# Eight-layer kernel on one core: three stretches reordered (start of the first layer, second expert layer with the attention behind it, last layer)

## The chip, the core and the metric

The kernel runs on one core of one Trainium2 chip, as one launch. Times are device microseconds of that core. The hardware profiler gives the busy time of each engine: TensorE (PE; PEld is its weight load), VectorE (DVE), ScalarE (ACT), GpSimd (POOL) and the queue that issues the transfers (SP).

## The reference

The input is 8 sequences of 256 tokens by 128 channels, float32. Eight layers are applied, each as `x = x + layernorm(f(layernorm(x)))`, with another f each time:

```python
f0: attention with a decaying prefix sum over cos/sin features (first layer, L0 attn)
f1: 8 experts, top 2, silu-gated                                (L0 ffn)
f2: 16-head softmax attention, with biases                      (L1 attn)
f3: (gelu(x @ W1[7] + b1[7]) @ W2[7] + b2[7]) * softmax(x @ Wr.T)[:, 7]      (L1 ffn)
f4: 16-head causal attention, polynomial in place of softmax    (L2 attn)
f5: a short attention over the sequences, then 8 experts, top 2, with a capacity (L2 ffn)
f6: causal softmax attention with one shared key head           (L3 attn)
f7: 16 experts in 4 groups: sigmoid scores; the 2 best groups by the sum of their 2 best
    scores; the 4 best experts in them, shares divided by their sum; silu(x@w1)*(x@w3)
    times the share, @ w2; plus a shared expert of width 128     (L3 ffn)
```

The three changed stretches are the start of f0, all of f3 with the start of f4, and all of f7. Everything is computed in float32, apart from the attention scores, whose operands are split into bf16 parts.

## The kernel before, in words

**Data.** `X` holds all tokens in SBUF, as 16 tiles of 128 tokens; a unit is one sequence, two tiles (T = 2), and there are NB = 8 units. All weights are loaded once at the start by SP, one pack per layer (`w_const`, `w_l0a`, `w_l0f`, ...; line 377), in this order: the first 4 tiles of X, const, l0a, the other 12 tiles of X, the bf16 constants in float32 (`cbf`, into PT), then the other packs.

**A unit of a layer.** The head: VectorE takes statistics of X (lines 1601 and 1604, semaphore hd_stat), GpSimd makes the inverse deviation (lines 395 and 397, hd_rstd), VectorE writes the normed state h (line 1611, hd_h), TensorE transposes it (line 896, hd_tr), ScalarE copies it out of PSUM (hd_hT). The layer's own work ends in an unnormed result. The tail: statistics (1617, 1620), GpSimd's inverse deviation again, the norm (1626) and the add to X (1629, semaphore x_done). Heads run one unit ahead.

**Order.** There is no scheduler: each engine has its own program, written out by hand, and runs it in order; semaphores, counted from the start, tie them together. A layer begins on TensorE once the last add of the layer before it is done (`pe.wait_ge(x_done, 1 + tail0[l])`). On VectorE every result that the next instruction reads needs an explicit `drain()` between.

**Start of the first layer.** GpSimd sets constants and clears the buffers of all the attentions (lines 405 to 420) and then raises `consts`, for which VectorE waits before its first statistics. VectorE norms unit 0, waits for the rest of X and for cbf, casts cbf (1702), then prepares the convolution weights `wcv` (1707 and 1712), the query weights `wab` (1709 to 1720), theta (1722) and the slopes, with one semaphore a_w for both weights. TensorE then runs the convolution (934) and the queries (943). VectorE computes exponents (1734, 1736) and angles (1742 to 1747), ScalarE copies the query factors (607), exponentiates (613) and takes sine and cosine (598 to 601), GpSimd multiplies them by the weights (551), TensorE makes running sums (957).

**Second expert layer (L1 ffn).** A hardware loop over the units on each engine. Only expert 7 is computed: hidden width 512 as two chunks of two 128-wide blocks. Per unit TensorE runs up(0), up(1) (line 1531, 256 columns each), then the transposes of the next unit's h, then down(0) and down(1) (line 1570) into one PSUM bank, and the next unit's router (1508). ScalarE does gelu (862), two copies of the next state (876, 879) and the exp of the router (845). VectorE begins with the next unit's h (1611), waits for down, adds the bias (2487), multiplies by the share (2491), takes the tail statistics, the head statistics of the unit behind, the router's maximum (1641, 1643), adds to X, and normalises the shares.

**Start of the third attention (L2 attn).** Behind the last add: projection of unit 0 (1241), loads from PSUM (1931 to 1933), and the splits of keys and queries into bf16 parts on VectorE (316 to 322, 332 to 338), their transposes (1248), copies, and the first scores (1266, 1255). In the loop of this attention GpSimd makes the splits.

**Last layer (L3 ffn).** A hardware loop again; five chunks per unit: chunk 0 the shared expert (width 128), chunks 1 to 4 four routed experts each. Per chunk TensorE runs up (1531), ScalarE silu (856), VectorE the product `y` (2437), TensorE the transposes of the spread shares `cwx` in PT (1542, function share), VectorE the product with the shares (2442), TensorE down (1570). The slots y, sg and the PSUM banks are doubled. The routing of the next unit stands between them on VectorE: sigmoid (2359, 2361), group scores (2364 to 2373), choice of groups (1668 to 1679, 2380 to 2388), comparison of 16 by 16 (1668 to 1674, 512 columns each), rank and shares (1679, 1682, 2394 to 2400, `cwn`). ScalarE spreads cwn over 64 columns each (871).

## Time and profile before

| | us |
|---|---|
| median of 3 runs | 1575.2 (1574.66 to 1577.04) |
| profiled execution, its own time | 1575.53 |
| its span | 1573.7 |
| TensorE busy in the span | 1217.3 |
| VectorE busy in the span | 1083.6 |
| ScalarE busy in the span | 737.8 |
| GpSimd busy in the span | 403.1 |

### The profile page before, as it was taken

Reading aid. Unit: us, or ns where it says so; the run is one execution under the profiler, and the core shown is the slowest. Engines: PE = TensorE matmul, PEld = TensorE weight load, DVE = VectorE, ACT = ScalarE, POOL = GpSimd, SP = SyncE. Lnnn points to the kernel's source line nnn. Section 1 sums busy time; section 2 is a strip of 40 time slices with the busy share of each in tenths; the row PEclk is TensorE's granted clock in tenths of the full one; section 3 lists DMA queues with packets and bytes.
Section 4 is the critical chain, followed back from the end, with each engine's and each line's share of the span. In section 5 each row is a group of like instructions: output and inputs, shape, how many; then the busy total and the mean of one; then the engine's idle time right before and its main releaser. Section 6 shows DMA issues by size and latency. Waiting matters only on the chain.

```text
span 1573.7 us, 27547 instructions
## 1 busy us (share of the span) xinstructions
PE 1217.3 (77%) x9120; PEld 853.1 (54%) x9120; DVE 1083.6 (69%) x3043; ACT 737.8 (47%) x1200; POOL 403.1 (26%) x622
## 2 busy tenths in 40 slices
PE   3989889999868777665678774877778999867876
PEld 2666658888733333454344442766663444456765
DVE  4788766666666777345788985788745666467777
ACT  3544523332326677553677772434233666524332
POOL 3545431000023332111545422222102223000000
PEclk8999989999958999777888995899886999969888
DMA  7000000000000000000000000000000000000000
GB/s 310 1 1 1 1 1 1 0 0 0 0 1 2 1 0 2 1 0 0 1 2 0 2 1 0 1 1 1 1 1 0 2 1 1 1 1 0 0 0 27
DMA packets 5688, 14.39 MB, mean 9 GB/s; under 512 B 224, under 2 KB 4448, under 8 KB 5088
## 3 DMA queue, kind: packets, MB, share of 16 engines
q1 hardware_dynamic: 5600, 13.26, 2.2%
q8 instruction: 49, 0.80, 0.2%
q14 instruction: 39, 0.32, 0.1%
HBM read 12.21 MB, written 1.05 MB: 8 GB/s over the span
## 4 chain that ended last, share of the span: by engine, by line
issue 51%; PE 20%; DVE 14%; POOL 5%; DVEq 4%; ACT 4%; POOLq 2%; DMA 1%; SPq 0%; ACTq 0%
PE PS L1116 3%; PE PS L1064 2%; PE PS L1058 2%; PE PS L1041 2%; POOL trs L397 2%; PE PS L1286 2%; PE PS L934 1%; DVE mx L1840 1%; POOLq L396 1%; DVE w_l0f L1950 1%; DVE sbuf L1747 1%; PE PS L957 1%; DVE h L1611 1%; PE PS L1022 1%; DVEq L1744 1%
## 5 line engine op out<-in xcount | busy, mean ns | idle before, releaser
L1840 DVE TENSOR_REDUCE mx<-PS 128x2 f32<-128x512 f32 (+1 forms) x256 | 155.0, 620 | 80.7 <-PE PS L1064 72.0
L672 ACT ACTIVATE w_l0f<-PS 128x512 f32<-128x512 f32 (+1 forms) x256 | 137.3, 543 | 100.4 <-PE PS L1071 97.7
L395 POOL TENSOR_TENSOR tve<-tmv,eps 128x2 f32<-128x2 f32 x64 | 12.6, 196 | 660.1 <-DVE tmv L1620 556.6
L856 ACT ACTIVATE sg<-PS 128x512 f32<-128x512 f32 (+1 forms) x104 | 60.4, 580 | 205.1 <-PE PS L1531 204.9
L1531 PE MATMUL PS<-hT_padded,w_l0f 128*128 128x256 f32 x512 | 121.7, 384 | 0.0
L896 PE MATMUL PS<-w_const,h 128*128 128x128 f32 x128 | 30.8, 328 | 104.5 <-DVE h L1611 95.0
L2437 DVE TENSOR_TENSOR y<-sg,PS 128x512 f32<-128x512 f32 (+1 forms) x104 | 69.3, 666 | 59.2 <-ACT sg L856 47.1
L1531 PEld LDWEIGHTS PS<-hT_padded,w_l0f 128*128 128x128 f32 x512 | 94.3, 193 | 10.8
L896 PEld LDWEIGHTS PS<-w_const,h 128*128 128x128 f32 x128 | 15.2, 154 | 126.7 <-DVE h L1611 86.0
L1531 PE MATMUL PS<-hT_padded,w_l3f 128*128 128x256 f32 x288 | 80.2, 432 | 0.0
L1444 PEld LDWEIGHTS PS<-w_l2f,y 128*128 128x128 f32 x512 | 72.0, 206 | 13.6 <-ACT y L789 8.8
L1444 PE MATMUL PS<-w_l2f,y 128*128 128x128 f32 x512 | 74.2, 292 | 6.5 <-ACT y L789 6.0
L1950 DVE SCALAR_TENSOR_TENSOR w_l0f<-w_l0f 128x768 f32<-128x768 f32 x64 | 67.5, 1054 | 15.3 <-ACT w_l0f L735 14.4
L1553 PE MATMUL PS<-w_l0f,y 128*128 128x128 f32 x512 | 69.1, 278 | 7.0 <-DVE y L2437 7.0
L1058 PE MATMUL PS<-w_cbf 128*128 128x384 bf16 x256 | 70.6, 345 | 4.6 <-DVE mx L1840 2.0
L735 ACT ACTIVATE w_l0f<-PS,one_c 128x768 f32<-128x768 f32 x64 | 58.2, 909 | 27.7 <-PE PS L1255 27.6
L1553 PEld LDWEIGHTS PS<-w_l0f,y 128*128 128x128 f32 x512 | 64.8, 191 | 11.2 <-DVE y L2437 8.8
L1611 DVE TENSOR_SCALAR h<-X,hmv,hrs 128x128 f32 (+1 forms) x112 | 55.0, 544 | 17.4 <-issue 9.6
L1531 PEld LDWEIGHTS PS<-hT_padded,w_l3f 128*128 128x128 f32 x288 | 61.8, 224 | 9.3
L1570 PE MATMUL PS<-w_l3f,y 128*128 128x128 f32 x288 | 46.2, 308 | 25.7 <-DVE y L2442 25.3
L789 ACT ACTIVATE y<-PS 128x512 f32<-128x512 f32 x64 | 37.4, 596 | 57.1 <-PE PS L1434 56.6
L1064 PE MATMUL PS<-KT,QT 56*128 56x256 bf16 (+1 forms) x256 | 50.7, 293 | 8.6 <-DVE mx L1840 4.5
(423 smaller groups left out, 3209.2 us busy)
## 6 DMA issues: line engine op xcount, KB each, us to landing
w_l0f<-in_l0f SPq DMA_DIRECT2D x1, 3076.0 KB, 13.8
w_l2f<-in_l2f SPq DMA_DIRECT2D x1, 2214.0 KB, 19.8
w_l3f<-in_l3f SPq DMA_DIRECT2D x1, 1736.0 KB, 23.5
w_l0a<-in_l0a SPq DMA_DIRECT2D x1, 1392.0 KB, 8.7
result<-X SPq DMA_DIRECT2D x1, 896.0 KB, 4.6
X<-in_x SPq DMA_DIRECT2D x1, 768.0 KB, 10.9
w_l1f<-in_l1f SPq DMA_DIRECT2D x1, 582.0 KB, 15.6
PT<-in_cbf SPq DMA_DIRECT2D x1, 576.0 KB, 11.9
```

What stands on the lines that cost most here:

```text
L672: act.activation(P8[:, hh % 8, 0:width], PS[:, hh % 2, 0:width], ACT.Exp, scale=SM_SCALE).then_inc(a["pt"], 1)
L735: act.activation(pair(PN[p]), PS[:, b:b + 2, 0:384], ACT.Identity, scale=-0.01 * SM_SCALE, bias=one_c[:]).then_inc(a["pn"], 1)
L856: act.activation(sg[:, c % 2, 0:cols], gate, func).then_inc(f["sg"], 1)
L1058: pe.matmul(PS[:, bank, 0:384], identb, w("cbf", mask), start=True, stop=False, skip_group_check=True)
L1064: return pe.matmul(PS[:, b, o], QTs[par][r:r + PARTS, hh // 2, t * P:(t + 1) * P], KTs[par][r:r + PARTS, 0 if causal else hh // 2, 0:o.sto ...
L1444: ins = pe.matmul(PS[:, 4 + c % 2, t * P:(t + 1) * P], y[:, c % 2, b * L + t * P:b * L + (t + 1) * P], w("l2f", "w2")[:, (2 * c + b) * D:( ...
L1531: ins = pe.matmul(PS[:, 2 * (c % 2) + g, b * L:(b + 1) * L], wt, hT[:], start=True, stop=True)
L1553: ins = pe.matmul(PS[:, 4 + c % 2, t * P:(t + 1) * P], y[:, c % 2, b * L + t * P:b * L + (t + 1) * P], w(name, "w2")[:, (2 * c + b) * D:(2 ...
L1611: ins = dve.tensor_scalar(h[:, t, :], src[:, bass.ds(u * T + t, 1), :].rearrange("p a b -> p (a b)"), hmv[:, t, 0:1], hrs[:, t:t + 1], ALU ...
L1840: dve.tensor_reduce(mx[:, hh, 0:nm], PS[:, 2 + hh % 2, 0:nm * keys].rearrange("p (t k) -> p t k", t=nm), AX.X, ALU.max).then_inc(a["mx"], 1)
L1950: dve.scalar_tensor_tensor(PN[p], PN[p], 2.0, PN[p], ALU.is_le, ALU.mult)
L2437: ins = dve.tensor_tensor(y[:, c % 2, 0:cols], sg[:, c % 2, 0:cols], PS[:, 2 * (c % 2) + 1, 0:cols], ALU.mult)
```

## The change

- **Start.** `wks`, `conv`, `slope`, `score` stand first in the pack l0a, which SP loads as two transfers: these 864 columns, then the other 1920. Then come cbf and only then the rest of X. `consts` is raised after the small memsets; those of KS, VA, KC, VC and cum follow GpSimd's first head_rstd. VectorE no longer waits for const before its first statistics (it does before logw), and makes wcv as soon as the first part is in, with a semaphore count of its own; the queries wait for a second count. cbf is cast after the angles of unit 0. ScalarE loads its exp table ahead (`warm(ACT.Exp)`), and copies the factors behind the first sine instead of before the exponents. The statistics and rstd of unit 1 stand before the loop.
- **Second expert layer.** Written out per unit instead of looped, as below. up(i), then the transposes of the state of i+2, down(i-1), router(i+2). The state copies go to three buffers in turn, the hidden values and the result's PSUM bank to two. Iteration NB-2 holds the next attention's first projection on TensorE, iteration NB-1 its load on VectorE; GpSimd splits its keys and queries there. What that attention did on VectorE, TensorE and ScalarE for this is removed.
- **Last layer.** Written out per unit. Three state buffers, four slots for the products (`cb` in place of y), the last two downs of a unit run under the next one's first chunks, ScalarE copies the result out of PSUM (`result_copy`), and VectorE's steps for three units (chunks of i, routing of i+1, head of i+2, tail of i-1) are interleaved so that fewer drains stand between.

```diff
@@ sync
             for n in PACKS:
-                sp.dma_start(W[n][:], packs[n]).then_inc(w_in[n], 16)
                 if n == "l0a":
+                    split = PACKS[n].at["wq_re"][0]
+                    sp.dma_start(W[n][:, 0:split], packs[n][:, 0:split]).then_inc(w_in[n], 16)
+                    sp.dma_start(W[n][:, split:], packs[n][:, split:]).then_inc(wb_in, 16)
+                    sp.dma_start(cbf_f[:, 0:PACKS_BF["cbf"].width], packs_bf["cbf"]).then_inc(wb_in, 16)
                     sp.dma_start(X[:, first:, :], xt[:, first:, :]).then_inc(x_rest, 16)
...
@@ gpsimd, l == L1_FFN
+                    head_rstd(head0[l] + 2)
+                    head_rstd(head0[l] + 3)
+                    for i in range(NB + 1):
+                        if i + 3 <= NB + 1:
+                            head_rstd(i + (head0[l] + 4))
+                        if there(i - 1):
+                            tail_rstd(i + tail0[l])
+                        if i == NB - 2:
+                            pool.wait_ge(behind["ld"], LOADS[L2_ATTN])
+                            pool.sem_inc(pool_turn, 1)
+                            split_keys(pool, L2_ATTN)
+                        if i == NB - 1:
+                            split_queries(pool, L2_ATTN, 0)
...
@@ scalar, l == L1_FFN
+                    gate_exp(0)
+                    state_copy(1)
+                    gate_exp(1)
+                    for i in range(NB):
+                        hidden(i)
+                        state_copy(i + 2)
+                        if there(i + 2):
+                            gate_exp(i + 2)
...
@@ tensor
-                if order[l]:
+                if l == L2_ATTN:
+                    pe.wait_ge(FF[L1_FFN]["oc"], NB)
+                elif order[l]:
                     pe.wait_ge(x_done, 1 + tail0[l])
...
@@ tensor, l == L3_FFN
+                    router(0)
+                    up(0, 0)
+                    state_transpose(1)
+                    router(1)
+                    for i in range(NB):
+                        for c in range(LAST_CHUNKS):
+                            if i or c:
+                                up(i, c)
+                            if c >= 2:
+                                down(i, c - 2)
+                            elif there(i - 1):
+                                down(i - 1, LAST_CHUNKS - 2 + c)
+                            if c:
+                                share(i, c)
+                            if c == 3 and there(i + 2):
+                                state_transpose(i + 2)
+                            if c == 4 and there(i + 2):
+                                router(i + 2)
...
@@ tensor, l == L1_FFN
+                    unit_ready(0)
+                    router(0)
+                    state_transpose(1)
+                    router(1)
+                    for i in range(NB):
+                        up(i)
+                        if i < NB - 1:
+                            state_transpose(i + 2)
+                        if there(i - 1):
+                            down(i - 1)
+                        if there(i + 2):
+                            router(i + 2)
+                        elif i == NB - 2:
+                            project_behind()
+                        else:
+                            pe.wait_ge(behind["ld"], LOADS[L2_ATTN])
+                            state_transpose(NB + 1)
+                    down(NB - 1)
...
@@ vector, l == L3_FFN, the last third of a unit
+                        gated(i, 3)
+                        if G:
+                            greater(msk[:], E16)
+                        dve.drain()
+                        shared_out(i, 3)
+                        if G:
+                            ties("rank16", E16)
+
+                        if S:
+                            logits(s)
+                        gated(i, 4)
+                        dve.drain()
+                        if G:
+                            beaten(E16)
+                        shared_out(i, 4)
+                        if D_:
+                            result_norm(i - 1)
+                        dve.drain()
+                        if G:
+                            ranked(rank[:], E16)
+                        if D_:
+                            result_add(i - 1)
+                        dve.drain()
...
@@ vector, l == L1_FFN
+                    for i in range(NB + 1):
+                        t, g, s, n = i - 1, i + 1, i + 2, i + 3
+                        if s == NB + 1:
+                            load_behind()
+                        if s <= NB + 1:
+                            head_norm(X, s % NB, s + (head0[l] + 1))
+                        if there(t):
+                            result(t)
+                        dve.drain()
+                        if there(t):
+                            result_share(t)
+                        if n <= NB + 1:
+                            state_stats(n)
+                        dve.drain()
+                        if there(t):
+                            result_stats()
+                        if n <= NB + 1:
+                            state_moments()
+                        dve.drain()
+                        if there(t):
+                            result_moments()
+                        if there(g):
+                            gate_sum(g)
+                        dve.drain()
+                        if there(g):
+                            gate_inverse()
+                        if there(s):
+                            gate_max(s)
+                        dve.drain()
+                        if there(g):
+                            gate_parts(g)
+                        if there(s):
+                            gate_less(s)
+                        dve.drain()
+                        if there(t):
+                            result_norm(t)
+                            dve.drain()
+                            result_add(t)
+                            dve.drain()
```

The L0 expert layer's code is only rewritten without its shared branches; its instructions stay.

## Rows read from the trace of the kernel before

**Rows 1.** Busy time by stretch: start:end, length, busy (x instructions) per engine, clock, DMA
```profile
0.00:33.00 33.00, 6.82 (x23) 5.94 (x24) 10.36 (x32) 11.10 (x19) 9.92 (x24) 0.90 0.94 368
662.00:731.00 69.00, 41.19 (x209) 36.88 (x207) 34.24 (x154) 36.07 (x63) 12.14 (x28) 0.83 0.00 0
731.00:760.00 29.00, 13.09 (x84) 7.38 (x88) 22.32 (x56) 9.33 (x13) 9.44 (x12) 0.66 0.00 1
953.00:1175.00 222.00, 159.74 (x945) 138.90 (x945) 162.85 (x610) 78.52 (x160) 51.04 (x112) 0.87 0.00 1
1400.00:1560.00 160.00, 126.69 (x700) 109.28 (x700) 116.43 (x379) 59.18 (x88) 12.16 (x28) 0.90 0.02 6
```

**Rows 2.** DMA issues: size and median us from issue to landing
```profile
w_l0a<-in_l0a SPq DMA_DIRECT2D x1, 1392.0 KB, 8.7
PT<-in_cbf SPq DMA_DIRECT2D x1, 576.0 KB, 11.9
```

**Rows 3.** Timeline of the start, 14 to 36 us: start, busy us, engine, line
```profile
14.68 0.76 DVE L1702 CAST w_cbf<-PT 128x1152 bf16<-128x1152 f32 x1 [5.21 <-DMA PT<-in_cbf]
...
16.09 0.29 DVE L1709 TENSOR_TENSOR coef<-w_l0a 128x128 f32<-128x128 f32 x1
...
18.45 4.60 PE L934 MATMUL PS<-wcv,hT_padded 128*128 128x160 f32 x16 [8.24 <-DVEq L1721]
...
27.94 0.61 ACT L598 ACTIVATE cb<-sbuf 128x512 f32<-128x512 f32 x1
...
32.49 2.08 PE L957 MATMUL PS<-cb,w_const 128*128 128x512 f32 x2 [8.42 <-POOL sbuf L551]
...
33.53 2.42 DVE L1611 TENSOR_SCALAR h<-X,hmv,hrs 128x128 f32<-128x128 f32 x2 [5.48 <-POOL hrs L397]
```

**Rows 4.** Routers by weight tile: records, ns min/median/max, first and last start
```profile
L1508 PE MATMUL PS<-w_l1f,hN x32: 175/256/361, 660.7 to 730.2; 128*128 128x8 f32 x32
L1508 PE MATMUL PS<-w_l1f,hT_padded x4: 353/361/361, 651.3 to 651.9; 128*128 128x8 f32 x4
...
L1508 PE MATMUL PS<-w_l3f,hN x32: 234/263/374, 1397.7 to 1552.7; 128*128 128x16 f32 x32
```

**Rows 5.** Timeline of one unit of the second expert layer
```profile
676.94 0.60 DVE L1611 TENSOR_SCALAR h<-X,hmv,hrs 128x128 f32 x2 [0.66 <-issue]
...
677.87 2.97 PE L1570 MATMUL PS<-w_l1f,y 128*128 128x128 f32 x16
...
683.18 0.69 POOL L397 TENSOR_TENSOR trs<-tve,mhalf 128x2 f32<-128x2 f32 x1
```

**Rows 6.** Timeline of the third attention's beginning
```profile
734.36 2.93 PE L1241 MATMUL PS<-w_l2a,hT_padded 128*128 128x384 f32 x4 [3.88 <-DVE X L1629]
...
748.17 0.50 PE L1266 MATMUL PS<-w_cbf 128*128 128x384 bf16 x2
...
752.53 0.82 POOL L316 CAST KS<-kf 128x768 bf16<-128x768 f32 x1 [2.60 <-DVE cb L1933]
...
762.46 1.10 POOL L338 TENSOR_TENSOR QS<-qf,QS 128x512 bf16<-128x512 f32 x1
```

**Rows 7.** Timeline of the last layer: first shares, and a stretch of one unit
```profile
1393.51 0.19 DVE L2400 TENSOR_TENSOR cwn<-msk,gsm 128x32 f32<-128x32 f32 x1 [0.43 <-issue]
...
1427.01 1.06 PE L1570 MATMUL PS<-w_l3f,y 128*128 128x128 f32 x8
...
1427.90 1.89 PE L1531 MATMUL PS<-hT_padded,w_l3f 128*128 128x256 f32 x8
...
1430.15 0.68 DVE L1668 TENSOR_TENSOR eqb<-msk 128x512 f32<-128x512 f32 x1
...
1430.75 0.68 DVE L1669 TENSOR_TENSOR gtb<-msk 128x512 f32<-128x512 f32 x1
...
1431.51 0.69 DVE L1671 TENSOR_TENSOR eqb<-eqb,w_const 128x512 f32<-128x512 f32 x1
```

**Rows 8.** Timeline of the end: the last add to X
```profile
1571.01 0.43 DVE L1629 TENSOR_TENSOR X<-X,tn 128x256 f32<-128x256 f32 x1
```

More of the change, by code:

```diff
@@ L350, in block_program @@
         shares_of = (cw, cwn)
+        LAST_CHUNKS = 5
+        last_hTs = (hT, hN[:], oT[:])
+        ones_state = last_hTs
+        hidden_of = lambda u, c: cb[:, 2 * (u % 2) + c]
+        Y1 = [PS[:, 5 + n, 0:L].rearrange("p (t d) -> p t d", t=T) for n in range(2)]
         def short(room, u):
@@ new lines, in _ @@
+                    dve.drain()
+                    ranked(gal[:], NG)
+                    dve.drain()
+                    groups_in()
+                    dve.drain()
+                    of_groups_in()
+                    dve.drain()
+                    below_the_rest()
+                    dve.drain()
+                    equal(msk[:], E16)
+                    greater(msk[:], E16)
+                    logits(1)
+                    dve.drain()
+                    ties("rank16", E16)
+                    dve.drain()
@@ new lines, in _, with unit @@
+                    take_shares()
+                    def unit(i, nxt, more):
+                        for c in range(1, E8):
+                            gated(i, c)
+                            if c == 1:
+                                head_norm(X, nxt, i + (head0[l] + 2))
+                            combine(i, c - 1)
+                            dve.drain()
+                            if c == 3:
+                                gate_less_max(f, GATE, i + 1)
+                            if c == 5:
+                                gate_share(f, i + 1, cwn)
+                            if c == 6:
+                                top_compare(cwn[:, :, 0:E8], E8, w("const", "rank8"))
+                        combine(i, E8 - 1)
+                        dve.drain()
+                        tail_stats(acc)
+                        if more:
+                            head_stats(X, (i + 2) % NB)
+                            gated(i + 1, 0)
+                        top_rank(cwn[:, :, 0:E8], E8, 2, cwn[:, :, 0:E8], rank[:, :, 0:E8])
+                        take_shares()
+                        tail_add(l, i, acc)
```

766 lines of the change are left out of this document (505 added, 261 removed).

## The prediction

> **What bounds the kernel now.** I read the windows first. The kernel runs eight layers one behind the other, each over eight units of 256 tokens, so its time is a sum of stages and a change is worth what it takes from its own. Three stretches are touched. In the first 33 us TensorE is busy 6.8 us and VectorE 10.4 us [rows 1]: everything waits for weights and preparation. In the second expert layer's loop (662 to 731) no engine reaches 60% (TensorE 41.2 of 69 us), and in the 29 us behind it TensorE works 13.1 us at a granted clock of 0.66. In the last layer's loop (1400 to 1560) TensorE works 126.7 us, VectorE 116.4, of 160 [rows 1]. Before is taken as its profiled execution: 1575.5 us, span 1573.7, so 1.8 us lie around the span; the median, 1575.2, is 0.3 lower.
>
> **Part 1, the beginning.** Now VectorE waits until 14.68 for the bf16 constants and casts them; only then come the convolution weights, from 16.09 the query weights, and the convolution runs 18.45 to 23.05; the first sine starts at 27.94 and the first running sum at 32.49 [rows 3]. The change cuts the layer's pack in two and loads the small part (864 of 2784 columns) first. The whole pack (1392 KB) landed 8.7 us after its issue at 1.8, at 10.5; the constants, with 768 KB of x ahead of them, at 14.6 [rows 2]. Behind the change only the pack's second part and the constants stand ahead (2.6 MB in place of 3.4), at these rows' slope of 3.1 us a MB about 12.2. The convolution needs only the first part (about 6.5), so with its 4.6 us at half clock it is over by about 12.5, under the second load. VectorE then does, from 12.2, what it did from 16.09 to the convolution's start, less the score product of 0.2 (2.15), then theta and slopes (1.1), exponents (0.45) and the first angles (2.0, while ScalarE weighs and loads its sine table): the first sine at 17.9 in place of 27.94, a lead of 10.0. Of the 4.9 us that lie between the convolution's end and the sine now, two copies and an exp table load on ScalarE are gone. The copies move behind it and stay under GpSimd, which weighs 2.5 us per chunk. The cast (0.76) moves to where VectorE waits for ScalarE. GpSimd's memsets of keys and values (some 4 us) go behind its first rstd and end long before it weighs. From 32.5 TensorE is nearly always busy, so its own lead is what counts: **10 us**. Bounds: 5, if the constants land at 14.6 as now and the copies were hidden; 14, if the loads shorten and the first unit's later waits close too.
>
> **Part 2, the second expert layer.** A unit takes 9.9 us: eight routers from 660.7, the last at 730.2 [rows 4]. In a unit, VectorE's norm of the next state (676.94) comes first, TensorE transposes it and only then runs the down products (677.87, 2.97 us), VectorE starts the result as they end (680.84), and the rstd follows at 683.18 [rows 5]. The new order keeps that piece: in iteration i the norm of unit i+2, its transposes, then down(i-1), and result(i-1) waits for it. So the new period is norm to down's start 0.93, down 2.97, then VectorE's row with interleaved drains up to where the rstd is needed (2.25), **two** rstds on GpSimd one behind the other, the head's now ahead of the tail's (2.0, by the row's 0.69 plus sum and gaps), then norm and add (1.2): 9.3 us. With down at full clock (1.9) it is 8.3. TensorE idles 3.5 to 4 us in a period, as now, so I take 9.1. ScalarE's two table loads and 1.6 us of gelu fit below that. The gelu, the up products and the router leave the chain, but the second rstd takes most of it back: 0.8 us a unit.
>
> The larger term is the join. Now the next attention's projection starts at 734.36 and its scores at 748.17 [rows 6]: 13.8 us, with splits of keys and queries on VectorE. After, the projection stands in iteration 6, VectorE's load in 7 (1.3 us), and the splits go to GpSimd, at 752.53 to 757.67 for keys and 4.9 us for queries up to 763.56 [rows 6], about twice VectorE's own. Queued behind them on GpSimd are the tails' rstds of units 6 and 7, and VectorE's last two results wait for those. From iteration 7's start T: keys split at T+6.4, rstd 7.5, queries 12.0, rstd 13.1, norm and add 14.3, VectorE's two copies 15.7, scores at T+15.9. T: the layer begins at 651.3 [rows 4], and the prologue and two thin iterations end at 671.9 (router 652.3, second state's norm 653, its router 656, up(0) at half clock 659.5, gelu 661, router(2) 662.3, down(0) 666.3, 5.6 of VectorE), then five periods of 9.1: 717.4. Scores at 733.3 in place of 748.2: **15 us**. Bounds: 10 with a period of 9.9, 19 with 8.3. Here VectorE and GpSimd work side by side; a norm of 0.60 us [rows 5] took 2.42 beside GpSimd at 33.53 [rows 3], and the split rows are already so slowed. The Trainium skill ("SBUF — State Buffer", Who interferes with whom) has a VectorE copy or tensor_scalar in a two-port mode and a GpSimd instruction shut each other out entirely; the 2.42 agrees. By it, VectorE's five such pairs in the last two iterations would cost up to 1.8 each, 9 us, were they not waiting for GpSimd anyway; I keep 15.
>
> **Part 3, the last layer.** A unit takes 22.1 us (first router 1397.7, the eighth's last record 1552.7, 7 intervals) [rows 4]. VectorE's instructions set the new one. Where nothing stands between, a 512-column instruction starts 0.60 us behind the last (1430.15, 1430.75); with a drain 0.76 (1431.51) [rows 7]; small ones by the same count 0.1 and 0.26. A unit has 13 of 512 columns (7.8), one of 256 (0.37), 24 small (2.6), and the statistics, norms and adds (2.55): 13.3. Drains now: 29, or 4.7 us, giving 18.0; the rest of 22.1 is waits and the loop. After: 21 drains, 3.4, **16.7**. TensorE, at full clock: 36 records of up products at 0.216 (7.8), 36 of down at 0.113 (4.05), by the starts at 1427.90 and 1427.01 and what follows them [rows 7]; 16 share transposes 1.7, the rest 0.6: 14.1. It fits, but in order: from shared chunk 2 it must do up(4), down(2), shares and router before VectorE gets its logits, which is 0.5 us longer than VectorE's work between. Period 17.2; with some stretches at 1.2 GHz, as the loop's mean clock of 0.90 shows [rows 1], 17.6. ScalarE gets a result copy (0.4) and has 8 us in all: nothing, as long as it waits behind gate(1). Loads: none moved. Sum: shares of unit 0 at 1395.2 (1.7 later than 1393.5 [rows 7], since unit 1's norm and logits stand in it), unit 0 16.2, five of 17.6, unit 6 15.5 (no head), unit 7 TensorE-bound with its tail 17.2: add at 1532. Now it ends at 1571.4 [rows 8]: **39 us**. Bounds: 47 (16.5 a unit) and 25 (19.5).
>
> **Sum.** 1575.5 - 10 - 15 - 39 = 1511.5; I say 1512.
>
> **Rivals.**
> - The pipelines hold their waits. The fourth expert layer is already interleaved by hand, and in its 222 us VectorE is busy 162.9 and TensorE 159.7 [rows 1]; were the last layer to fill as badly, its 16.1 us of busy VectorE a unit (116.4 of 160, of 22.1) would need 21.9: part 3 keeps only what the ends give, 9. Then 1575.5 - 10 - 15 - 9 = 1542. Against it: there 8 chunks wait for each other, here VectorE alone fills 95%. Chance 0.07.
> - TensorE's clock. Its work before the logits has no slack, so a fall to 1.2 GHz behind the 2.3 us that it waits for the spread shares goes straight into the period. At a clock of 0.8 on that path: 19.5 to 20 a unit, 25 us for part 3, total 1525. For: the present loop has 0.90. Against: its waits of 3.3 us go. Chance 0.17.
> - Parts 1 and 2 at their lower bounds (5 and 10): 1521. Chance 0.13.
> - The saved drains save nothing. The mechanism: an instruction without a drain would still wait for the last one's end, so the 8 drains saved come back and VectorE needs 18.0; period 18.9, about 9 us less, 1521. The Trainium skill ("VectorE: DVE Perf Modes", The DRAIN you can't avoid) says that the flush comes after every operation and that only their number counts. The rows disagree: 0.68 us long, yet the next starts after 0.60 [rows 7]. Chance 0.03.
> - Slower than before: TensorE falls to 1.2 GHz for the whole last layer, since it now waits in many small gaps. Then it needs 28.2 us a unit, 6.1 more than now: 8 units, +49, less 25 from parts 1 and 2, 1599. It decides where the mean clock falls below 0.56 (14.1/0.56 = 25.2, three us above now). The loop's 0.90 at 79% busy speaks against. Chance 0.02.
>
> **The numbers.** The forecast has 0.55; 0.03 lies below 1503, with all at the upper bounds. The range 1500 to 1530 takes in the forecast, the clock, the lower bounds and the drains. A measurement tells some 0.2% (3 us) from no change. Faster 0.96, within 0.02, slower 0.02.
>
> **What would show it.** Step 1: the first running sum at about 22.5. Step 2: the distance of two h norms in the second expert layer near 9.1, two rstds back to back on GpSimd ahead of tn, first scores 15.9 behind the load. Step 3: VectorE busy above 88% in the last layer, lg waiting about half a us for PE, cwn 17.6 apart. It is wrong if cwn stand 19 apart or more, if GpSimd's splits delay the join past T+18, or if the first sine waits for a load.

## The result, and the profile after

The changed kernel takes **1510.7 us** (median of 4 runs, 1508.2 to 1514.2) against 1575.8 for the kernel before beside it: a ratio of 0.9585, with a 95% interval of 0.9572 to 0.9599, or 65 us. The forecast was 1512. The profiled execution took 1508.2 us with a span of 1506.4, 67.3 less than before's 1573.7.

Where they went is read from the first records of the layers. Before and after: first router of the first expert layer 233.7 and 221.4; of the second 651.3 and 638.5; first projection of the third expert layer (f5; the prediction calls it the fourth) 958.1 and 931.8; first router of the last layer 1383.0 and 1354.7. So the start gave 12.3 us, the second expert layer and the attention behind it 13.5 (306.8 to 293.3 between these points), the last layer 39.0 (190.7 to 151.7 to the span's end); the other 2.5 lie in layers that the change does not touch, 1.4 of them in the last attention (206.8 to 205.4).

These are one trace of each kernel, and the traces of the experiments below, 13 in all, show how far a stretch scatters with its instructions unchanged. The old start ends at 231.9 to 233.7 in three traces, the new one at 221.4 to 222.6 in seven: 10.4 us between the middle values. The last layer as changed takes 151.7 us in three traces and 153.8 or 153.9 in four, the old one 189.3 to 191.3: 36.9 between the middle values. So the 12.3 pair the slowest trace of the old start with the fastest of the new, and the 39.0 a middle one of the old last layer with a fast one of the new. The last attention is at 206.7 or 206.8 in the three traces without the new second expert layer and at 205.3 to 205.8 in the ten with it; why is open.

Busy time by stretch in the changed kernel (start:end, length, PE, PEld, DVE, ACT, POOL, granted clock, DMA); the first, second and last answer to [rows 1]:

```profile
0.00:33.00 33.00, 17.33 (x65) 12.43 (x66) 23.82 (x45) 16.30 (x29) 16.98 (x29) 0.84 0.95 368
638.00:708.00 70.00, 46.56 (x228) 39.82 (x228) 32.07 (x155) 33.78 (x61) 13.03 (x30) 0.80 0.00 1
1380.00:1490.00 110.00, 94.14 (x601) 85.35 (x600) 92.29 (x311) 51.30 (x76) 11.85 (x22) 1.00 0.00 1
```

The start is fuller now (VectorE busy 72% of it for 31%), and the last layer went from 79% to 86% on TensorE and from 73% to 84% on VectorE, at full clock. The second expert layer is still far from full on any engine: its units came down only from 9.9 to 9.35 us (661.07 to 698.48 in the starts of h norm, four units), and 9.54 to 9.67 in the five other traces with this order. Most of its gain is in the join.

**The start**, timeline (start, busy us, engine), against [rows 3]:

```profile
5.61 1.80 POOL L434 MEMSET KS<- 128x2048 bf16 x1
...
5.71 2.75 DVE L1871 TENSOR_SCALAR h<-X,hmv,hrs 128x128 f32<-128x128 f32 x2 [1.15 <-POOL hrs L412]
...
9.83 4.60 PE L1024 MATMUL PS<-wcv,hT_padded 128*128 128x160 f32 x16 [0.64 <-DVE wcv L1881]
...
11.16 0.29 DVE L1886 TENSOR_TENSOR coef<-w_l0a 128x128 f32<-128x128 f32 x1 [0.71 <-DMA PT<-in_cbf]
...
16.93 0.61 ACT L643 ACTIVATE cb<-sbuf 128x512 f32<-128x512 f32 x1
...
21.82 2.08 PE L1047 MATMUL PS<-cb,w_const 128*128 128x512 f32 x2 [6.52 <-POOL sbuf L592]
```

The constants land at 11.1 and set what follows: coefficients at 11.16, the first sine at 16.93 (from 27.94), the first running sum at 21.82 (from 32.49). One row stands out: the h norm takes 2.75 us beside GpSimd's fill of KS, where it took 0.60 before, beside none. The convolution, which waits for it, ends at 14.4, just when VectorE has made the weights and takes it up (la at 14.49, without a wait).

**One unit of the second expert layer**, against [rows 5]:

```profile
688.78 0.60 DVE L1793 TENSOR_SCALAR h<-X,hmv,hrs 128x128 f32<-128x128 f32 x2 [0.17 <-issue]
...
689.43 0.44 PE L1669 MATMUL PS<-w_const,h 128*128 128x128 f32 x2 [3.92 <-DVE h L1793]
...
689.71 3.22 PE L1697 MATMUL PS<-w_l1f,cb 128*128 128x128 f32 x16
...
692.97 0.42 DVE L2818 TENSOR_TENSOR acc<-PS,w_l1f 128x256 f32<-128x256 f32 x1 [3.59 <-PE PS L1697]
...
695.49 0.69 POOL L412 TENSOR_TENSOR hrs<-hve,mhalf 128x2 f32<-128x2 f32 x1
...
696.48 0.69 POOL L412 TENSOR_TENSOR trs<-tve,mhalf 128x2 f32<-128x2 f32 x1
...
697.21 0.60 DVE L2837 TENSOR_SCALAR tn<-acc,tmv,trs 128x128 f32<-128x128 f32 x2 [1.09 <-POOL trs L412]
...
697.88 0.43 DVE L2841 TENSOR_TENSOR X<-X,tn 128x256 f32<-128x256 f32 x1
```

The chain is whole: h norm, transposes, down products at half clock, result, statistics, two rstds, norm, add. TensorE stands idle for 3.9 us ahead of the transposes while it could have done the down products; VectorE waits 3.6 us for them, then 1.09 for the second rstd.

**The join**, GpSimd, one row of VectorE and the first scores, against [rows 6]. VectorE's load from PSUM begins at 707.60:

```profile
709.05 0.82 POOL L314 CAST KS<-kf 128x768 bf16<-128x768 f32 x1 [2.68 <-DVE vf L2869]
...
716.18 1.10 POOL L336 TENSOR_TENSOR QS<-qf,QS 128x512 bf16<-128x512 f32 x1
...
716.18 1.38 DVE L2823 TENSOR_SCALAR acc<-acc,cwn 128x128 f32<-128x128 f32 x2
...
718.52 0.19 POOL L410 TENSOR_TENSOR tve<-tmv,eps 128x2 f32<-128x2 f32 x1 [1.24 <-DVE tmv L2831]
...
722.13 0.50 PE L1357 MATMUL PS<-w_cbf 128*128 128x384 bf16 x2 [1.49 <-DVE QT L2119]
```

The scores start 14.5 us behind the load, 83.6 us behind the layer's first router; before it was 96.9. The last row of GpSimd shows that its splits no longer held the chain at its end: it waits 1.24 us for VectorE's statistics, after a share product on VectorE that took 1.38 us beside the split at 716.18, in place of 0.48.

**The last layer.** The first shares (cwn) are computed at 1366.92, then at 1384.96, 1402.30, 1419.43, 1436.82, 1453.94, 1471.07 and 1486.99. An undisturbed unit takes 17.13 us; two of 17.34 and 17.39 hold a stall of 0.43 us which the profile calls issue. Two such stretches, columns as above:

```profile
1402.30:1419.43 17.13, 14.69 (x97) 13.39 (x95) 14.89 (x51) 8.11 (x12) 2.12 (x4) 1.00 0.00 0
1419.43:1436.82 17.39, 14.94 (x97) 13.41 (x95) 14.88 (x52) 8.11 (x12) 2.12 (x4) 1.00 0.00 1
```

And all of VectorE's waits in the five middle units (total us, times, longest):

```profile
DVE lg L2533 <- PE PS L1599: 2.6, 5, 0.6
DVE ex L2540 <- issue: 0.4, 1, 0.4
DVE gal L2576 <- issue: 0.4, 1, 0.4
```

VectorE waits 0.5 us a unit for its logits and, but for the two stalls, for nothing else.

### The profile page after: what moved, and what is told of

Same layout as the page of the kernel before. It is cut to its first block, busy times and chain, and to the rows that moved or that the text cites. A ratio compares the mean times of both kernels' runs of the same rounds, so it can differ in the third digit from the quotient of the medians.

```text
span 1506.4 us, 26816 instructions
## 1 busy us (share of the span) xinstructions
PE 1193.8 (79%) x9110; PEld 837.2 (56%) x9110; DVE 1064.8 (71%) x2986; ACT 724.5 (48%) x1182; POOL 411.6 (27%) x628
## 4 chain that ended last, share of the span: by engine, by line
issue 49%; PE 21%; DVE 14%; POOL 6%; ACT 4%; DVEq 4%; POOLq 3%; ACTq 0%
PE PS L1207 3%; PE PS L1155 2%; PE PS L1149 2%; PE PS L1132 2%; POOL trs L412 2%; PE PS L1377 2%; DVE mx L2021 1%; PE PS L1047 1%; POOLq L411 1%; PE PS L1024 1%; POOL hrs L412 1%; DVE w_l0f L2131 1%; DVE sbuf L1923 1%; PE PS L1113 1%; PE PS L1046 1%
## 5 line engine op out<-in xcount | busy, mean ns | idle before, releaser
L1752 PEld LDWEIGHTS PS<-hT_padded,w_l0f 128*128 128x128 f32 x512 | 94.5, 193 | 10.7
L966 ACT ACTIVATE sg<-PS 128x512 f32<-128x512 f32 x64 | 38.2, 597 | 116.7 <-PE PS L1752 116.6
L410 POOL TENSOR_TENSOR hve<-hmv,eps 128x2 f32<-128x2 f32 x65 | 17.0, 261 | 243.2 <-DVE hmv L1786 108.8
L2950 DVE TENSOR_TENSOR y<-sg,PS 128x512 f32<-128x512 f32 x64 | 44.0, 688 | 49.7 <-ACT sg L966 42.1
L1761 PE MATMUL PS<-w_l0f,y 128*128 128x128 f32 x512 | 69.1, 278 | 6.9 <-DVE y L2950 6.9
L984 PE MATMUL PS<-w_const,h 128*128 128x128 f32 x94 | 22.2, 323 | 49.9 <-DVE h L1793 40.5
L1793 DVE TENSOR_SCALAR h<-X,hmv,hrs 128x128 f32<-128x128 f32 (+1 forms) x110 | 53.8, 543 | 3.2 <-issue 2.1
L1155 PE MATMUL PS<-wB,wA 56*128 56x256 bf16 (+1 forms) x256 | 47.1, 268 | 9.3 <-DVE mx L2021 7.8
L412 POOL TENSOR_TENSOR hrs<-hve,mhalf 128x2 f32<-128x2 f32 x65 | 50.1, 771 | 9.3
L643 ACT ACTIVATE cb<-sbuf 128x512 f32<-128x512 f32 x24 | 15.1, 630 | 70.3 <-DVE sbuf L1923 70.0
## 6 DMA issues: line engine op xcount, KB each, us to landing
w_l3f<-in_l3f SPq DMA_DIRECT2D x1, 1736.0 KB, 22.6
```

Of the source, the lines that this page charges most:

```text
L412: pool.tensor_tensor(rs[:], ve[:], mhalf[:], ALU.pow).then_inc(ready, 1)
L1155: return pe.matmul(PS[:, b, o], QTs[par][r:r + PARTS, hh // 2, t * P:(t + 1) * P], KTs[par][r:r + PARTS, 0 if causal else hh // 2, 0:o.sto ...
L1752: ins = pe.matmul(PS[:, 2 * (c % 2) + g, b * L:(b + 1) * L], w("l0f", "w1")[:, at:at + P], hT[:], start=True, stop=True)
L1761: ins = pe.matmul(PS[:, 4 + c % 2, t * P:(t + 1) * P], y[:, c % 2, b * L + t * P:b * L + (t + 1) * P], w("l0f", "w2")[:, (2 * c + b) * D:( ...
L1793: ins = dve.tensor_scalar(h[:, t, :], src[:, bass.ds(u * T + t, 1), :].rearrange("p a b -> p (a b)"), hmv[:, t, 0:1], hrs[:, t:t + 1], ALU ...
```

## The experiments

All ran beside the kernel before; times are medians.

**Each part alone.** Three kernels, each the kernel before with the lines of one part:

```diff
+                    sp.dma_start(W[n][:, 0:split], packs[n][:, 0:split]).then_inc(w_in[n], 16)
...
```
```diff
+                if l == L1_FFN:
+                    behind = AT[L2_ATTN]
...
```
```diff
+                elif l == L3_FFN:
+                    f = FF[l]
...
```

Part one takes the pack's order, the split load and all that is moved in the first layer; part two the branches of L1_FFN and the third attention's beginning; part three the branches of L3_FFN.

> The kernel before with the first attention's other beginning alone. If the parts add up and what the start gives is kept by all layers behind it, the time is 12 to 12.5 us under the kernel before (1563), with the first running sum at 21.8 us and every later layer earlier by the same; my prediction had 10. If a pipeline behind the start holds a wait that swallows part of it (the first rival), the distance has shrunk below 6 us by the second layer and the time is 1570 or more.

Measured 1565.2 (ratio 0.9943, 0.9921 to 0.9965). First router of the first expert layer at 221.8, of the second at 641.8, of the last at 1373.8. So 11.9 us are won at the first mark and 9.2 are left at the last, less than the 12 to 12.5 expected. Of the 2.7 lost, 2.5 go in the second attention, which this kernel does not touch, and which is as slow in part two's trace with the old start (below): it is not this start that costs them. The swallowing rival, with under 6 us left by the second layer, falls.

> The kernel before with the second expert layer's pipeline and the third attention that begins in it. Theory: period 9.35 us, the first scores 14.5 us behind the load, and so 13 us (12 to 14.5) under the kernel before, 1562.5. Rival: the third attention waits later for what was not prepared (its second unit's state), so that part of the 13 is given back inside that layer: the distance at the routers of the next layer is under 8, the time over 1567.

Measured 1562.0 (0.9915, 0.9886 to 0.9944). Between the second expert layer's router and the third's projection lie 294.0 us, 12.8 fewer than before's 306.8. The gain is kept through the attention. The same untouched stretch takes 307.1 us in part one's trace but 311.1 in part three's, so its old value is itself known only to some 4 us.

> The kernel before with the slots of the last layer alone. Theory: period 17.2 us and 39 us (38 to 40.5) under the kernel before, 1536.5; the rest of the program is untouched. Rival: part of the 39 came from the clock, which stood at full speed in the last layer only because the work ahead of it was shifted; then the granted clock of the last layer is under 0.95 here, the period 18 or more and the time over 1541.

Measured 1540.1 (0.9774, 0.9741 to 0.9807), 34 us by the medians and 36 by the ratio, between what the two expected. The last layer takes 153.9 us here (36.8 fewer); its units are as in the changed kernel, at full clock:

```profile
1397.24:1415.86 18.62, 15.95 (x86) 14.34 (x87) 13.66 (x44) 7.83 (x11) 0.88 (x2) 0.82 0.00 0
1415.86:1432.98 17.12, 15.52 (x103) 14.19 (x101) 14.86 (x51) 8.11 (x12) 2.12 (x4) 1.00 0.01 1
1432.98:1450.11 17.13, 14.69 (x97) 13.38 (x95) 14.86 (x52) 8.11 (x12) 2.12 (x4) 1.00 0.00 1
```

The clock rival does not hold. Of the 2.2 us more in this layer, 0.6 lie in the first unit and 1.7 behind the last shares, and three later traces with this same layer, in kernels that hold all three parts, take 153.8 too. The three ratios add to 58 us (9.0, 13.4 and 35.6, each uncertain by 3.5 to 5), the change gives 65; that is within their scatter, and the traces' own stretches add to 61.5.

One source of that scatter shows in the traces. The second attention, from its first projection to the second expert layer's router, has the same instructions in all kernels, yet takes 220.4 (before), 219.9 (changed) and 220.3 us (part three alone) in some traces and 222.9 and 222.5 (parts one and two alone) in others, with 160 and 162.3 us of busy TensorE and a mean clock of 0.84 and 0.83. Over all 13 traces it runs from 217.4 (both orders, 156.3 us of busy TensorE, clock 0.87) to 222.9. As each kernel left one trace, chance and a lasting effect of the other layers are not told apart. Single traces can't be compared closer than some 5 us; a stretch within them can only as far as it is seen to repeat.

**Drains put back.** In a unit of the last layer eight more, such as:

```diff
                         gated(i, 0)
+                        dve.drain()
                         if G:
                             plus_one(g)
```

> The changed kernel with 8 more drains in each unit of the last layer, put between neighbours of a slot that do not need one. If each drain on VectorE costs the 0.16 us that my step priced and VectorE sets the period, a unit is 1.3 us longer (18.4 to 18.5 us from shares to shares) and the kernel 9 to 10 us slower than the changed one (1520). If the next instruction waits for an empty pipe anyway (the Trainium skill, VectorE: DVE Perf Modes, The DRAIN you can't avoid: there a drain in place of the wait is nearly free), the period stays at 17.2 and the time at 1511. If TensorE sets the period instead, VectorE's 1.3 us go into its idle time and the period grows by less than 0.4 us.

Measured 1522.9 (0.9671, 0.9644 to 0.9698), 12 us slower than the changed kernel, where 9 to 10 were expected. Shares to shares, middle units:

```profile
1388.96:1407.59 18.63, 16.06 (x103) 14.26 (x101) 15.66 (x52) 8.11 (x12) 2.13 (x4) 1.00 0.01 1
1407.59:1426.88 19.29, 16.35 (x97) 14.63 (x95) 15.74 (x52) 8.12 (x12) 2.13 (x4) 0.91 0.00 0
1426.88:1445.15 18.27, 15.21 (x97) 13.43 (x95) 15.64 (x51) 8.11 (x12) 2.13 (x4) 1.00 0.00 1
1445.15:1464.11 18.96, 16.36 (x97) 14.63 (x95) 15.66 (x51) 8.12 (x12) 2.13 (x4) 0.91 0.01 1
```

The mean over seven is 18.46, 1.31 more, just what eight drains at 0.16 give. That is chance: the first unit grew by 0.17 and the seventh, at a clock of 0.90, by 1.68. Unit by unit it is two things: at full clock 18.27 against 17.13, 1.14 more (eight drains of 0.16, less what the wait for the logits gave back: 0.31 in this unit in place of some 0.5), and in every second unit 0.7 to 1.0 on top, with the mean clock at 0.91. VectorE's row does set the period. The Trainium skill ("VectorE: DVE Perf Modes", The DRAIN you can't avoid) says that the next operation does not start until the pipe is empty, by which the period would be unchanged, and adds that a next operation which is not held starts earlier. The measurement agrees with the addition: here a drain between two instructions that don't need one costs 0.14 us of period.

**The second expert layer, down products first.**

```diff
                         up(i)
-                        if i < NB - 1:
-                            state_transpose(i + 2)
                         if there(i - 1):
                             down(i - 1)
+                        if i < NB - 1:
+                            state_transpose(i + 2)
```

> The changed kernel, but in the second expert layer TensorE does the down projection of unit i-1 ahead of the transposes of the state of unit i+2. My step priced the period of this layer as one chain: h norm, transposes, the 16 matmuls of the down projection, result, statistics, rstd, norm, add. If that chain is what holds it, the 3.6 us in which VectorE waits for the down projection go, and TensorE's own row is the next bound: ups 2.0, down 3.2, transposes 0.44, copy 0.4, router 0.7, so 6.8 us a unit in place of 9.35, 16 to 18 us in all: 1493.5. Rival: the state's chain (h norm, transposes, copy, router, exponential with its two table loads, Gelu) holds the period as well, since its transposes now come up to 3.2 us later: then the period is over 8.5 and the gain under 7 us.

Measured 1498.6 (0.9520, 0.9504 to 0.9536), 12 us under the changed kernel, where 16 to 18 were expected; in the trace the layer up to VectorE's load is shorter by more (from its first router to the copy of the values 69.5 us in the changed kernel, 54.6 here: 14.9), and router to the third expert layer's projection by 16.1. From add to add the units take 6.37, 7.00, 6.01, 6.99 and 6.00; two of them, with the columns of the first stretches:

```profile
666.51:673.51 7.00, 6.50 (x48) 5.84 (x46) 4.36 (x21) 4.95 (x9) 1.73 (x4) 1.00 0.00 0
673.51:679.52 6.01, 4.29 (x16) 3.47 (x17) 4.26 (x22) 4.69 (x9) 1.73 (x4) 0.77 0.00 0
```

The state's chain doesn't hold the period, the order of two steps on TensorE did. The bound is not a plain 6.8 either: units near 7.0, in which VectorE still waits 0.9 us for the down products, alternate with units near 6.0, VectorE's own row with its wait of 1.09 us for the second rstd. The profiled execution is the fastest of its four (1491.3, the others 1497 to 1501), so the trace shows some 5 us more than the medians do.

**The result's rstd first.**

```diff
-                        if i + 3 <= NB + 1:
-                            head_rstd(i + (head0[l] + 4))
                         if there(i - 1):
                             tail_rstd(i + tail0[l])
+                        if i + 3 <= NB + 1:
+                            head_rstd(i + (head0[l] + 4))
```

> The changed kernel, but in the second expert layer GpSimd takes the rstd of the result ahead of that of the state. Theory: VectorE's wait of 1.09 us for it falls to about 0.4, the state's rstd is still there before it is used, and each of the 7 full periods is 0.65 us shorter: 4 to 5 us in all (1506). Rival: the order of the two is even, since the next h norm then waits for the other: period 9.35 and 1511 as before.

Measured 1510.4 (0.9585, 0.9568 to 0.9602), no different from the changed kernel. In the trace the step did what was expected: the wait for trs fell from 1.09 to 0.42, and router to copy of the values from 69.5 to 64.8, 4.7 us.

```profile
687.78 0.60 DVE L2837 TENSOR_SCALAR tn<-acc,tmv,trs 128x128 f32<-128x128 f32 x2 [0.42 <-POOL trs L412]
```

But the attention behind it took 226.7 us from there to the third expert layer's projection, against 223.8 in the changed kernel, and the second attention 222.4, in front of the edit. The local gain is shown. The 226.7 lie outside the 222.3 to 224.2 of the five other traces with the old order of the rstds and the down products (part two, drains put back, and the three last single edits below), but the kernel with both orders has 223.5; whether the edit gives the 2.9 back is open.

**Both orders.**

> Both orders turned. If TensorE is the bound once the down projection stands first, the rstd's order is then worth nothing and the time is that of that kernel, within 1.5 us; if VectorE's chain is still the bound, 4 to 5 us less than with the down projection first alone.

Measured 1496.3 (0.9502, 0.9486 to 0.9517). From add to add the units take 5.72, 6.99, 5.35, 5.54 and 5.36; the last four:

```profile
663.57:670.56 6.99, 6.52 (x44) 5.98 (x43) 4.38 (x22) 4.74 (x9) 1.73 (x5) 0.91 0.00 0
670.56:675.91 5.35, 4.04 (x27) 3.41 (x26) 4.29 (x21) 4.63 (x9) 1.73 (x5) 1.00 0.00 0
675.91:681.45 5.54, 4.85 (x35) 4.22 (x33) 4.38 (x22) 4.64 (x9) 1.74 (x5) 1.00 0.00 0
681.45:686.81 5.36, 4.44 (x24) 3.33 (x23) 4.11 (x20) 2.30 (x6) 1.73 (x5) 1.00 0.02 5
```

The second of the two: with the down products out of the way the chain is VectorE's, with GpSimd's rstd in it, and the rstd's order is worth 0.65 a unit (6.00 to 5.35); router to copy goes to 50.6, 4.0 less than with the down products first alone. In the last three TensorE, fuller, is at full clock and busy under 5 us. In the unit of 6.99, at a clock of 0.91, VectorE still waits 1.54 us for the down products; with all four edits (below) no such unit is left. In the whole time 2.3 of the 4.0 show, at the edge of what the runs tell.

**Fills behind the second rstd.** The block of memsets of KS, VA, KC and VC moves behind the second head_rstd:

```diff
-                if order[l] == 0:
-                    pool.memset(KS[:], 0.0)
...
                     head_rstd(head0[l] + 2)
+                    pool.memset(KS[:], 0.0)
...
```

> The changed kernel, but GpSimd fills the attention's buffers behind its second rstd, not beside VectorE's first h norm. The h norm took 2.75 us beside the fill of KS, against 0.60 elsewhere. If the fill is the cause, it takes 0.6 to 0.7 us here and the first convolution begins 1.0 to 1.3 us sooner; the first sine is held by the constants' landing at 11.1 us and the coefficients behind them and moves by under 0.4 us, so the whole time stays within 1 us. [...] The first coefficients now lie beside the fills: if they slow by as much, the first sine is later by 1 to 3 us.

Measured 1512.6, one run. The start:

```profile
5.62 0.60 DVE L1869 TENSOR_SCALAR h<-X,hmv,hrs 128x128 f32<-128x128 f32 x2 [1.15 <-POOL hrs L412]
...
8.43 4.61 PE L1022 MATMUL PS<-wcv,hT_padded 128*128 128x160 f32 x16 [1.46 <-DVE wcv L1879]
...
10.98 0.29 DVE L1884 TENSOR_TENSOR coef<-w_l0a 128x128 f32<-128x128 f32 x1 [1.94 <-DMA PT<-in_cbf]
...
13.13 1.18 DVE L1895 TENSOR_SCALAR wA<-w_l0a 128x1024 f32<-128x1024 f32 x1
```

The norm is back at 0.60, the convolution 1.4 us sooner, and all of it is hidden under the constants' landing; the product wA, now beside a fill, takes 1.18 in place of 0.69, and the first sine is 0.3 later, which is within what the start scatters (16.93 to 17.64 in seven traces). The fill is the cause: the norm takes 0.60 in all three traces with the fills behind it. For a tensor_scalar, which can run in a two-port mode, the Trainium skill ("SBUF — State Buffer", Who interferes with whom) says that it and a GpSimd instruction shut each other out entirely, and both rows agree with that; the coefficients' tensor_tensor stay at 0.29 beside the fills.

The changed kernel's own trace is the mild case. In four of the seven traces with its start the norm took 3.7 us, and in three of these VectorE then waited for the convolution, here with the drains put back:

```profile
5.66 3.73 DVE L1871 TENSOR_SCALAR h<-X,hmv,hrs 128x128 f32<-128x128 f32 x2 [1.16 <-POOL hrs L412]
...
15.16 0.23 DVE L1910 TENSOR_SCALAR la<-PS 128x64 f32<-128x64 f32 x1 [0.65 <-PE PS L1024]
```

So the fills beside the norm cost up to 0.65 us of the start, if not in every execution.

**The start's wait split.** The fills as in the last experiment, and VectorE waits for the bf16 constants only at the cast:

```diff
-                    dve.wait_ge(wb_in, 32)
+                    dve.wait_ge(wb_in, 16)
...
+                            dve.wait_ge(cbf_in, 16)
                             dve.tensor_copy(W["cbf"][:], cbf_f[:, 0:PACKS_BF["cbf"].width]).then_inc(cbf_ready, 1)
```

> The changed kernel, but VectorE waits for the bf16 constants only at their cast, not ahead of the coefficients, and GpSimd fills later. Theory: the coefficients wait for the second part of the pack alone, which landed 7.3 us after its issue against 8.4 for the constants, and begin near 10.1 in place of 11.16 us; the first convolution is over by 13.1, so the first sine is 0.8 to 1.1 us earlier (16.0) and the first running sum at 20.9. Rival: the two loads share the engines and land together, so that splitting the wait gives nothing; or the cast's wait comes to stand in the way.

Measured 1510.3, one run. Coefficients at 9.54, first sine at 16.06, first running sum at 20.95, first router of the first expert layer at 220.5 (221.4): as expected, 0.9 us, too small for the whole time. In the changed kernel the coefficients did wait 0.71 us for a load of 576 KB that nobody needs yet. But they came 1.6 us sooner here and the sine only 0.9: wA, beside a fill, took 1.46 us. And with all four edits, which hold this one, wA took 1.87, the sine came at 16.94 and the router at 221.8, inside the 221.4 to 222.6 of the unchanged start. So the wait is gone, and that it is worth 0.9 us rests on one trace.

**The router ahead in the last layer.**

```diff
                                 up(i, c)
+                            if c == 4 and there(i + 2):
+                                router(i + 2)
                             if c >= 2:
                                 down(i, c - 2)
```

> The changed kernel, but in the last layer TensorE does the router of unit i+2 right behind the fifth up projection, ahead of the third down projection and the fourth shares. My step gave 0.5 us of each period to VectorE's wait for the logits and the rest to VectorE's own row. If so, that wait is gone, the period is 16.6 to 16.7 us (from 17.16) and the kernel 3.5 to 4 us shorter than the changed one. Rival: TensorE's order has no room anywhere (it is busy 86% of the time), the delayed down projection and shares make VectorE wait 0.5 us later in the unit, and the period stays at 17.1 to 17.2.

Measured 1511.9 (0.9587, 0.9567 to 0.9606): nothing gained, mean period 17.16. Shares to shares:

```profile
1406.44:1424.09 17.65, 15.60 (x93) 14.14 (x92) 15.06 (x52) 8.12 (x12) 2.13 (x4) 0.90 0.00 0
1424.09:1440.91 16.82, 15.26 (x101) 13.89 (x99) 14.78 (x51) 8.12 (x12) 2.13 (x4) 1.00 0.00 1
1440.91:1458.57 17.66, 15.61 (x93) 14.05 (x91) 15.14 (x52) 8.11 (x12) 2.13 (x4) 0.90 0.01 1
1458.57:1475.03 16.46, 14.90 (x101) 13.79 (x99) 14.78 (x51) 8.12 (x12) 2.13 (x4) 1.00 0.01 1
```

Neither theory. At full clock a unit takes 16.46 (16.82 with a stall of 0.43): the 0.67 us hang on the logits as priced, TensorE's order has the room. But every second unit falls to a mean clock of 0.90, and its 17.65 give it all back. The fall, in the timeline of TensorE:

```profile
1408.72 0.66 PE L1622 MATMUL PS<-w_const,PT 128*128 128x128 f32 x4 [2.05 <-ACT PT L899]
1409.21 3.01 PE L1612 MATMUL PS<-oT,w_l3f 128*128 128x256 f32 x8
```

Busy time and granted clock of a stretch in it:

```profile
1409.70:1412.90 3.20, 3.20 (x12) 2.70 (x11) 2.73 (x13) 0.60 (x1) 0.00 (x0) 0.52 0.00 0
```

The eight up products take 3.01 us, not 1.89: for some three microseconds TensorE runs at its lower level of 1.2 GHz (granted clock 0.52), after 2.05 us of waiting for the spread shares. In the changed kernel it waits as long there (2.06) and stays at 2.4 GHz; in the units of this kernel that stay at 2.4 GHz it waits 1.56. Why it falls in the one and not the other the runs don't settle.

**All four edits.**

> The changed kernel with the four edits: in the second expert layer the down projection ahead of the transposes and the result's rstd ahead of the state's (together 1496.3 us), the router ahead in the last layer, and the start's wait split. If each is worth here what it was alone, 3.5 to 4.5 us below the 1496.3 of the first two: 1492 (1490 to 1495). Rival: the third attention or TensorE's clock takes back what comes early, as may have happened to the rstd's order alone, and the time stays at 1496.

Measured **1493.4** (5 runs, 1490.6 to 1497.4; 0.9485, 0.9472 to 0.9498): 17 us under the changed kernel, 82 under the kernel before. Nearly all of it is the second expert layer, whose units run at 5.36 and 5.52. The last layer alternates between 16.8 and 17.65 as with the router ahead alone, so that edit is worth nothing here either. Against the first two edits' 1496.3, 2.9 us less lies within the scatter, so the rival that the time stays at 1496 is not ruled out.

## Why the prediction was right, step by step

The number was right (1510.7 against 1512), and so were most steps; some errors cancelled, and that each part's gain in the one trace lies so near its forecast is in part luck, as the scatter of the same stretches shows.

- **Part 1, 10 us: 12.3 in the trace, 11.9 alone, 10.4 by the middle values.** Constants at 11.1 for 12.2, first sine at 16.93 for 17.9, first running sum 21.82 for 22.5. The term that was mis-sized is the landing, 1.1 sooner. It was the base more than the slope: the pack's second part, with the same 2.0 MB down to it as the whole pack before, landed at 9.5 (2.24 and 7.3) and not at 10.5, and the constants 1.6 behind it. In the other traces with this start they land at 11.1 to 11.8. The convolution was not over by 12.5 but at 14.4, 1.4 us of it because the fills slowed the norm ahead of it; the prediction had the fills cost nothing, and only VectorE's own row, as long, hid it. Of the 1.6 us between the running sum's gain (10.7) and the layer's (12.3), 0.9 are the first unit's later waits, which I had left to the bound (its last product H begins at 30.15 for 41.72), and the rest comes later in the layer. The sign "if the first sine waits for a load" was half met: the sine itself does not, the coefficients ahead of it do, as the sum had it.
- **Part 2, the unit, 9.1: 9.35.** The chain was named rightly, and its prices by clock were 8.3 and 9.3; the unit at full clock takes 8.43, those with the down products at half clock 9.3 to 9.95. The load begins 69.1 us behind the first router, for 66.1: 2.0 of the 3.0 lie in the prologue and the two thin iterations (22.6 for 20.6), which I had priced too quickly, 1.0 in the periods. And the chain was of the order's making: the two orders turned cut it to 5.35.
- **Part 2, the join, 15.9 behind the load: 14.5.** GpSimd's key splits took 3.4 us (709.05 to 712.46) and not 5.1: the prices were taken from rows in which it worked beside VectorE's 768-column products. So the layer's part is 13.3 us from router to scores, not 15: 3.0 lost up to the load, 1.4 won behind it. That VectorE's slowed pairs cost nothing, as they wait for GpSimd anyway, held until the last result: there GpSimd waited 1.24 us for VectorE.
- **Part 3, 39 us: 39.0.** First shares 12.2 us behind the router, as forecast. Period 17.2 at full clock: measured 17.13. The allowance for the clock, to 17.6, was not needed in the middle units, at 1.00 throughout: the five took 86.1 for 88.0. It was needed in the first (18.04 for 16.2, clock 0.84), which I had priced without. The seventh took 15.9 for 15.5, the last with its tail 16.7 for 17.2 (last add at 1503.73). In all 136.8 us from first shares to last add for 136.9: errors of nearly 2 us each way that cancelled. One sign failed: VectorE was to be busy above 88% of the last layer and was at 84% of the 110 us above, 87% of a unit (14.89 of 17.13); the forecast "VectorE alone fills 95%" counted its 3.4 us of drains in full, while eight drains put back, some 1.3 us, added only 0.77 us of busy time (14.89 to 15.66).
- **The term of 0.5 for the logits** is in the trace, and with the router ahead a unit at full clock is shorter by 0.67.
- **The drains** are worth what [rows 7] gave, 0.16; the rival that they save nothing falls.
- **The pipelines hold their waits:** in the last layer VectorE waits 0.5 us a unit, so no. (The layer that this rival was priced on, at 953 to 1175, is the third of the four expert layers, not the fourth.) In the second expert layer, though, this rival was half right: there the new pipeline did hold two waits, of 3.6 and 1.09 us.
- **TensorE's clock** did not decide here, but it is near: one step moved, or VectorE slowed by 1.1 us a unit, and every second unit falls. The chance of 0.17 was for a real thing.

## What to carry to other kernels

When a pipeline is written out by hand, look at each engine's order for a step whose inputs have long been there behind one that has to wait; here one such swap on TensorE was worth about as much as the pipeline and the join together had brought. Read periods unit by unit, with the granted clock beside each: a mean that fits the price of an edit may be a smaller price plus a clock that falls in every second unit. And a gain in the middle of a chain of layers should be measured from one fixed record to the next, since the untouched layers scatter by up to 5 us; where it can be had, from more than one trace.

## What was not expected of the hardware

- Taking a wait of half a microsecond from VectorE, or giving it eight drains more, each brought TensorE down to 1.2 GHz for some three microseconds in every second unit, where the changed kernel's order kept 2.4 GHz in all but the first.
- A GpSimd fill, which reads nothing, holds a VectorE tensor_scalar: 2.75 or 3.7 us in place of 0.60 for the norm, 1.18 to 1.87 in place of 0.69 for the 1024-column product.
- The same instructions of an untouched attention take 217.4 to 222.9 us in 13 traces, at mean clocks of 0.87 to 0.83.
